# Local attention: per-head norms on four 64x64 matmul tiles, their inverses put back across partition halves, and the softmax sums ahead of the normalisation

## The chip, the core and the metric

The kernel runs on one core of a Trainium2 chip, in float32. The metric is the device time of one execution in microseconds (us); a run of the kernel is one such time, and the table below gives the median of three. One execution was also recorded by the hardware profiler, and all rows shown here come from that one. The engines are TensorE (PE; its weight loads are listed as PEld), VectorE (DVE), ScalarE (ACT), GpSimd (POOL) and SyncE (SP), which issues the DMAs.

## What is computed

The reference is a sandwich of four residual blocks on a tensor of 8 sequences x 256 tokens x 128 channels: additive attention, a six-layer local attention with a gated feed-forward layer, a state space layer, and a mixture of experts. The change lies in the local attention alone. Cut to what matters, one of its six layers is:

```python
q, k, v = split(shift_tokens(x) @ Wqkv)          # 16 heads of 64
q = l2norm(q) * q_scale                          # each head's 64 values
k = l2norm(k) * k_scale
q = q * cos * scale + rotate_half(q) * sin * scale
k = k * cos / scale + rotate_half(k) * sin / scale
sim = einsum(q, look_back(k)) * 8                # windows of 32, own and previous
out = softmax(mask(sim)) @ look_back(v)
x = out @ Wo + x
x = (a * gelu(gate)) @ W2 + b2 + x               # a, gate from layer norm, W1
```

The sum of squares of a head's 64 values, and its inverse root, are what the change is about.

## The kernel before

Everything is kept transposed: channels on the 128 partitions, tokens along the free dimension. The local attention works on chunks of 512 tokens (two batches of 256, called b = 0 and 1; four chunks per layer, 24 in all) and, within a chunk, on eight pairs of heads j = 0 to 7. A pair fills the 128 partitions: one head on partitions 0 to 63, the other on 64 to 127. Queries and keys of a pair lie side by side, 512 columns each, with q first.

Each engine has its own function `slot(i, m, j, run, more, before)`, called for every chunk i and pair j in the same order by `iterations` (a loop over layers, unrolled four chunks deep, with the first and last chunks written out). An iteration below is one chunk, eight slots. The order of the calls inside `slot` is the order of that engine's queue, written out by hand; engines meet only through semaphores. The work is staggered: in slot j the scores of pair j are made, the projection and norms of pair j + 2, the transposes of pair j - 1 and the value mix of pair j - 2. The output projection and the feed-forward layer of the chunk before are spread over the slots: Wo in slots 0 to 2 (three, three and two matmuls), the layer norm's mean in slot 3 and variance in slot 4, the gate and hidden matmuls at the end of slot 5, in slot 6 and at its end, W2 in slot 7.

The steps of one pair, with the lines of the profile:

- `project` (TensorE, L470, L471): Wq and Wk times the tokens, into PSUM banks 0 and 1, 512 columns each. It waits until the Ln of the pair before has read these banks. `values` (L459) makes part of the values on two 128x64 tiles.
- `raw_copy` (ScalarE, L646, L649): copies both banks to `raw`, then writes the squares to `sq`.
- `swap` (SyncE, L405): two DMAs copy `raw` to `shuf` with neighbouring partitions exchanged.
- `norms` (TensorE, L477, L478): two matmuls of the 128x128 matrix `same_head` (ones where two channels belong to one head) with `sq`, so that each partition holds its head's sum of squares, again in banks 0 and 1.
- `inverse_norm` (ScalarE, L655, L657): Ln of both banks into `rn`, then Exp with scale -0.5 and the bias operand `con.lift`.
- `straight` (GpSimd, L749, L753): the first step, `raw` times the cosine table, overwrites `rot`, so it waits for the normalisation of the pair before; the second step adds `shuf`, which `rotate` (VectorE, L778) has by then multiplied by the sine table.
- `normalise` (VectorE, L785): `rn` times `rot` into `qk`, which the scores read.
- `scores` (TensorE, L489 and L497): two mask matmuls, then 32 small matmuls on 64x32 tiles, into banks 4 and 5, one bank for each half of the rows.
- `soft_a` (VectorE, L793, L797): maximum and difference; the exponent (ScalarE, L699); `soft_b` (VectorE, L804, L807, L809): sums, reciprocal, product.
- `turn` (TensorE, L507): four transposes; `spread` (ScalarE, L664, L665, L667): three copies into `ptz`; `mix` (TensorE, L520): 16 matmuls on four 64x64 tiles into banks 6 and 7, one bank for each half of the rows; `out_copy` (ScalarE, L674).

In the ScalarE queue of a slot the order is exponent, raw copy, squares, output copy, value copy (L639), the layer norm's parts (L696 ahead of the exponent and L711, L713 in slot 4, L716 in slot 5), Ln, Exp, spread; the gelus and two table loads stand at the start of slot 6. In the VectorE queue it is `soft_a`, `normalise` of pair j + 1, `soft_b`, then the residual and layer norm parts, then `rotate` of pair j + 2. On TensorE, `need` attaches a wait to the next instruction; `gather` makes the wait an instruction of its own:

```python
def gather(sm_, value):
    if not isinstance(value, int) or value > 0:
        pe.wait_ge(sm_, value)
        pe.sem_inc(sem["seen"], 1)
```

An fp32 matmul appears in the profile as two records, each with its own weight load.

Of the kernel before, what the change touches and what calls it, by code (L numbers as in the profile page):

```python
# [21 lines left out]
ACT = mybir.ActivationFunctionType  # L22
AX = mybir.AxisListType

B, S, C = 8, 256, 128
T = B * S
CH = 512
# [5 lines left out]
UNIT = 512  # L33
# [11 lines left out]
def view(buf, col, *pattern, p0=0, rows=128):  # L45

    a = buf[p0:p0 + rows, 0:1]
    return bass.AP(a.tensor, a.offset + col, [[a.ap[0][0], rows]] + [list(x) for x in pattern])
# [240 lines left out]
def need(eng, sem, value):  # L289

    if not isinstance(value, int) or value > 0:
        eng.wait_ge(sem, value)


def local_attention(nc, io, x, con):
# [9 lines left out]
    with Pool(nc) as m:  # L305
# [3 lines left out]
        ps = m.mem.enter_context(nc.psum_tensor("f_ps", [128, 8 * CH], F32))  # L309
# [4 lines left out]
        fcol = m.sb("f_fcol", 9)  # L314
        base_c, base_s = m.sb("f_basec", 2 * S), m.sb("f_bases", 2 * S)
        tab_c, tab_s = m.sb("f_tabc", 2 * S), m.sb("f_tabs", 2 * S)
        same_head, ident = m.sb("f_same", C), m.sb("f_ident", C)
# [2 lines left out]
        identb = m.mem.enter_context(nc.sbuf_tensor("f_identb", [128, C], mybir.dt.bfloat16))  # L320

        v = m.sb("f_v", 8 * CH)
        raw, sq, shuf, rot, rn = (m.sb(f"f_{n}", 2 * UNIT) for n in ("raw", "sq", "shuf", "rot", "rn"))
        KOFF = UNIT + WIN
        qk = [m.sb(f"f_qk{b}", KOFF + UNIT) for b in range(2)]
        s = [m.sb(f"f_s{b}", UNIT) for b in range(2)]
# [6 lines left out]
        sem = {n: m.sem("f_" + n) for n in (  # L333
            "const wv0 wv1 wqk0 wqk1 wo w1 w2 zero flat v_mm v a_mm raw sq n_mm ln rn shuf turned straight rot qk s_mm max "
            "shift exp sum rcp p t_mm ptz pv_mm o wo_mm y1 mean cen sq2 var ln2 rs2 scaled xn g_mm gelu h_mm hid "
            "w2_mm y2 fcol tab seen").split()}
        bank = lambda k, n=1: view(ps, k * CH, *([[CH, n]] if n > 1 else []), [1, CH])


# [103 lines left out]
        def _(pe):  # L443
# [29 lines left out]

            def norms(i, j):

                need(pe, sem["sq"], i * 8 + j + 1)
                pe.matmul(bank(0), same_head[:, :], sq[:, 0:UNIT], start=True, stop=True)  # L477
                pe.matmul(bank(1), same_head[:, :], sq[:, UNIT:], start=True, stop=True).then_inc(sem["n_mm"], 1)  # L478

            def scores(i, j):  # L480

# [151 lines left out]
        def _(act):  # L633
# [17 lines left out]
            def inverse_norm(i, j):  # L651

                need(act, sem["n_mm"], i * 8 + j + 1)
                need(act, sem["qk"], i * 8 + j)
                act.activation(view(rn, 0, [UNIT, 2], [1, UNIT]), bank(0, 2), ACT.Ln, scale=float(2.0 ** 20)).then_inc(sem["ln"], 1)  # L655
                need(act, sem["ln"], i * 8 + j + 1)
                act.activation(rn[:, :], rn[:, :], ACT.Exp, scale=-0.5, bias=con.lift).then_inc(sem["rn"], 1)  # L657

            def spread(i, j):

# [102 lines left out]
        def _(dve):  # L763
# [48 lines left out]
            def hidden(i, f):  # L812

                n = FB[f][1]
                need(dve, sem["h_mm"], i * 3 + f + 1)
                need(dve, sem["gelu"], i * 3 + f + 1 + G0)
                dve.scalar_tensor_tensor(out=hid[0:n, f * UNIT:f * UNIT + UNIT], in0=view(ps, 3 * CH, [1, CH], rows=n),
                                         scalar=fcol[0:n, 2 + f:3 + f], in1=gate[0:n, f * UNIT:f * UNIT + UNIT],
                                         op0=ALU.add, op1=ALU.mult).then_inc(sem["hid"], 1)

            def slot(i, m, j, run, more, before):
# [7 lines left out]
                    hidden(k, 0)  # L829
                if before and j == 7:  # L830
                    hidden(k, 2)
                if next1:
                    normalise(u1, a1)
                if j == 6 and more and m == NU - 1:
                    tables(i + 1)
                if run:
                    soft_b(i, j)
                if before and j == 6:
                    hidden(k, 1)
                if before and j == 2:  # L840
                    need(dve, sem["wo_mm"], k + 1)
                    for g in range(2):
                        ins = dve.tensor_tensor(tokens(mk, g), tokens(mk, g), pair_of(ps, 3 * CH, 64 * g, 64), ALU.add)
# [25 lines left out]
            for t in qk:  # L869
                mm = dve.memset(t[:, UNIT:KOFF], 0.0)  # L870
# [820 lines left out]
```

## Time and profile before

| | |
|---|---|
| three runs | 2463.16, 2466.7, 2469.34 us (median 2466.7) |
| profiled execution | 2463.6 us, span 2461.8 us |
| mean granted TensorE clock | 0.971 of full speed |
| TensorE busy | 2236.4 us (91% of the span) |
| ScalarE busy | 1762.5 us (72%) |
| VectorE busy | 1596.1 us (65%) |
| GpSimd busy | 1082.4 us (44%) |
| weight loads (PEld) | 1067.3 us (43%) |

The local attention lasts from about 100 to 1925 us of the span. Its iterations take 75.6 us each with little scatter, so one iteration can stand for all. Times in a timeline are microseconds from the start of the span; busy time says that an instruction was under way, and matmul records overlap, so a busy TensorE need not be at its full rate.

### The profile page before, as it was taken

To read this page: it belongs to the slowest core of one execution; us is meant where nothing else is said; L and a number is where in the kernel's file an instruction comes from. 1 tells how busy PE (TensorE), PEld (TensorE's weight loads), DVE (VectorE), ACT (ScalarE), POOL (GpSimd) and SP (SyncE) were. 2 spreads that over 40 slices of the span, in tenths; PEclk is the share of its full clock that TensorE was granted. 3 is DMA by queue.
4 is the path that set the end of the run, shared out by engine and by line. 5 is a ranking of instruction groups with operands and counts; after the bars stand their busy time and mean duration, and the time that the engine had idled before them with its cause. 6 is when DMAs were issued, how large, how long until landed. Compare 5 with 4: busy or idle time off the path is not lost. (4 is left out here: it accounts for less than half of the span.)

```text
span 2461.8 us, 60471 instructions
## 1 busy us (share of the span) xinstructions
PE 2236.4 (91%) x24172; PEld 1067.3 (43%) x24172; DVE 1596.1 (65%) x2054; ACT 1762.5 (72%) x2574; POOL 1082.4 (44%) x461
## 2 busy tenths in 40 slices
PE   8789999999999999999999999999999687777787
PEld 3244444444444444444444444444444222222355
DVE  5556666566665666666666666766666489998442
ACT  4578877788777887777887787877787465455533
POOL 0354454444544445445454444454544015566030
PEclk8899999999999999999999999999999889999789
DMA  0211111111111112111121111211111100000001
GB/s 22 100 61 54 59 68 74 63 61 61 75 66 71 61 54 87 53 71 62 53 87 63 70 53 62 79 70 62 61 53 53 40 1 0 0 0 0 19 26 43
DMA packets 46753, 130.34 MB, mean 53 GB/s; under 512 B 9760, under 2 KB 12208, under 8 KB 46384
## 3 DMA queue, kind: packets, MB, share of 16 engines
q1 hardware_dynamic: 46480, 126.47, 13.6%
q8 instruction: 199, 3.26, 0.6%
q14 instruction: 74, 0.61, 0.1%
HBM read 24.73 MB, written 1.05 MB: 10 GB/s over the span
## 5 line engine op out<-in xcount | busy, mean ns | idle before, releaser
L749 POOL TENSOR_TENSOR f_rot<-f_raw,f_tabc 128x1024 f32<-128x1024 f32 x192 | 452.4, 2356 | 593.8 <-ACT f_raw L646 506.6
L753 POOL TENSOR_TENSOR f_rot<-f_rot,f_shuf 128x1024 f32<-128x1024 f32 x192 | 453.6, 2363 | 396.2 <-DVE f_shuf L778 396.2
L778 DVE TENSOR_TENSOR f_shuf<-f_shuf,f_tabs 128x1024 f32<-128x1024 f32 x192 | 235.4, 1226 | 306.7 <-DMA f_shuf<-f_raw 306.0
L655 ACT ACTIVATE f_rn<-f_ps 128x1024 f32<-128x1024 f32 x192 | 196.5, 1024 | 270.9 <-PE f_ps L478 270.9
L785 DVE SCALAR_TENSOR_TENSOR f_qk<-f_rn,f_rot 128x1024 f32<-128x1024 f32 x192 | 234.2, 1220 | 61.8 <-POOL f_rot L753 58.8
L477 PE MATMUL f_ps<-f_sq,f_same 128*128 128x512 f32 x384 | 205.1, 616 | 64.1 <-ACT f_sq L649 61.3
L793 DVE TENSOR_REDUCE f_max<-f_ps 128x8 f32<-128x512 f32 x192 | 132.6, 691 | 186.2 <-PE f_ps L497 185.0
L657 ACT ACTIVATE f_rn<-f_rn,k_lift 128x1024 f32<-128x1024 f32 x192 | 220.6, 1149 | 6.3
L646 ACT ACTIVATE f_raw<-f_ps 128x1024 f32<-128x1024 f32 x192 | 197.0, 1026 | 38.6 <-PE f_ps L471 37.3
L470 PE MATMUL f_ps<-y_t,f_wq 128*128 128x512 f32 x384 | 218.2, 650 | 0.6 <-ACT f_rn L655 0.4
L1172 POOL TENSOR_TENSOR s_prod<-s_state,s_cs 128x1024 f32<-128x1024 f32 x64 | 151.8, 2371 | 146.8 <-DVE s_state L1250 146.8
L459 PE MATMUL f_ps<-f_wv,y_t 128*64 128x512 f32 x768 | 208.9, 622 | 5.2 <-issue 5.2
L649 ACT ACTIVATE f_sq<-f_raw 128x1024 f32<-128x1024 f32 x192 | 203.0, 1057 | 6.1
L520 PEld LDWEIGHTS f_ps<-f_ptz,f_v 64*64 64x64 f32 x6144 | 136.2, 133 | 156.8 <-issue 156.8
L478 PE MATMUL f_ps<-f_sq,f_same 128*128 128x512 f32 x384 | 197.5, 596 | 0.0
L471 PE MATMUL f_ps<-y_t,f_wk 128*128 128x512 f32 x384 | 196.8, 594 | 0.0
L533 PE MATMUL f_ps<-f_o,f_wo 128*128 128x512 f32 x384 | 183.8, 611 | 0.0
L520 PE MATMUL f_ps<-f_ptz,f_v 64*64 64x96 f32 (+1 forms) x6144 | 162.7, 244 | 5.1 <-ACT f_ptz L667 5.1
L497 PE MATMUL f_ps<-f_qk 64*32 64x64 f32 x12288 | 165.4, 225 | 0.0
L1250 DVE TENSOR_TENSOR_SCAN s_state<-s_ps,s_state 128x1024 f32<-128x1024 f32 x64 | 146.6, 2290 | 15.0 <-ACT s_ps L1121 14.8
L1121 ACT ACTIVATE s_ps<-s_delta,s_aneg 128x1020 f32<-128x1020 f32 x64 | 71.4, 1115 | 115.5 <-DVE s_state L1250 110.1
L497 PEld LDWEIGHTS f_ps<-f_qk 64*32 64x32 f32 x12288 | 134.2, 106 | 40.8 <-issue 40.8
(264 smaller groups left out, 3684.0 us busy)
## 6 DMA issues: line engine op xcount, KB each, us to landing
f_shuf<-f_raw SPq DMA_DIRECT2D x384, 256.0 KB, 2.4
e_w<-in_e_w SPq DMA_DIRECT2D x16, 256.0 KB, 2.9
f_wq<-in_f_wq SPq DMA_DIRECT2D x12, 256.0 KB, 2.9
f_wk<-in_f_wk SPq DMA_DIRECT2D x12, 256.0 KB, 3.3
f_wv<-in_f_wv SPq DMA_DIRECT2D x12, 256.0 KB, 3.6
f_wo<-in_f_wo SPq DMA_DIRECT2D x6, 512.0 KB, 3.4
f_w<-in_f_w SPq DMA_DIRECT2D x6, 341.0 KB, 3.2
s_dx<-in_k_pick SPq DMA_DIRECT2D x1, 1536.0 KB, 9.0
```

Of the source, the lines that this page charges most:

```text
L459: mm = pe.matmul(view(ps, 2 * CH, [1, CH], p0=64 * b, rows=64), y[:, at:at + 64], wv[:, CH * (q // 4):CH * (q // 4) + CH], start=True, sto ...
L470: pe.matmul(pair_of(ps, 0), wq[:, 128 * j:128 * j + 128], shifted(m), start=True, stop=True)
L477: pe.matmul(bank(0), same_head[:, :], sq[:, 0:UNIT], start=True, stop=True)
L478: pe.matmul(bank(1), same_head[:, :], sq[:, UNIT:], start=True, stop=True).then_inc(sem["n_mm"], 1)
L497: mm = pe.matmul(view(ps, (4 + h) * CH + (2 * four + b) * 64, [1, 64], p0=WIN * (w % 4), rows=WIN), t[64 * h:64 * h + 64, WIN * w:WIN * w ...
L520: mm = pe.matmul(view(ps, (6 + b) * CH + S * b + 64 * p, [1, n], p0=64 * h, rows=64), v[64 * b:64 * b + 64, p * INNER + 128 * j + 64 * h:p ...
L649: act.activation(sq[:, :], raw[:, :], ACT.Square).then_inc(sem["sq"], 1)
L657: act.activation(rn[:, :], rn[:, :], ACT.Exp, scale=-0.5, bias=con.lift).then_inc(sem["rn"], 1)
L749: pool.tensor_tensor(view(rot, 0, [S, 4], [1, S]), view(raw, 0, [S, 4], [1, S]), view(tab_c, 0, [S, 2], [0, 2], [1, S]), ALU.mult).then_in ...
L753: pool.tensor_tensor(rot[:, :], rot[:, :], shuf[:, :], ALU.add).then_inc(sem["rot"], 1)
L778: dve.tensor_tensor(view(shuf, 0, [S, 4], [1, S]), view(shuf, 0, [S, 4], [1, S]), view(tab_s, 0, [S, 2], [0, 2], [1, S]), ALU.mult).then_i ...
L785: dve.scalar_tensor_tensor(out=view(qk[j % 2], 0, [KOFF, 2], [1, UNIT]), in0=view(rn, 0, [UNIT, 2], [1, UNIT]), scalar=1e12, in1=view(rot, ...
```

## The change

It has three parts. In `norms`, the two full matmuls become eight of 64x64: for q and k (t), for each batch (b), and for each head of the pair (h), the 64x64 block of ones times that head's 64 rows of squares, 256 columns. Batch 0's sums go to the head's own half of the partitions in bank 0; batch 1's go to the *opposite* half, in bank 1. The wait for the squares becomes a `gather`. In `inverse_norm`, `rn` is twice as wide; the Ln still covers 1024 columns; the Exp is split into one instruction for batch 0 (512 columns, 128 partitions) and two for batch 1 (512 columns, 64 partitions each), which read one half of the partitions and write the other, so that the inverse norms are back where `normalise` expects them. In the VectorE `slot`, `soft_b` of pair j comes ahead of `normalise` of pair j + 1. A semaphore named `cross` is declared and not used.

```diff
-        raw, sq, shuf, rot, rn = (m.sb(f"f_{n}", 2 * UNIT) for n in ("raw", "sq", "shuf", "rot", "rn"))
+        raw, sq, shuf, rot = (m.sb(f"f_{n}", 2 * UNIT) for n in ("raw", "sq", "shuf", "rot"))
+        rn = m.sb("f_rn", 4 * UNIT)
...
             def norms(i, j):
 
-                need(pe, sem["sq"], i * 8 + j + 1)
-                pe.matmul(bank(0), same_head[:, :], sq[:, 0:UNIT], start=True, stop=True)
-                pe.matmul(bank(1), same_head[:, :], sq[:, UNIT:], start=True, stop=True).then_inc(sem["n_mm"], 1)
+                gather(sem["sq"], i * 8 + j + 1)
+                for t in range(2):
+                    for b in range(2):
+                        for h in range(2):
+                            to = 64 * h if b == 0 else 64 - 64 * h
+                            mm = pe.matmul(view(ps, CH * b + S * t, [1, S], p0=to, rows=64),
+                                           same_head[64 * h:64 * h + 64, 64 * h:64 * h + 64],
+                                           sq[64 * h:64 * h + 64, UNIT * t + S * b:UNIT * t + S * b + S], start=True, stop=True)
+                mm.then_inc(sem["n_mm"], 1)
...
                 need(act, sem["n_mm"], i * 8 + j + 1)
                 need(act, sem["qk"], i * 8 + j)
-                act.activation(view(rn, 0, [UNIT, 2], [1, UNIT]), bank(0, 2), ACT.Ln, scale=float(2.0 ** 20)).then_inc(sem["ln"], 1)
+                act.activation(view(rn, 0, [UNIT, 4], [1, S]), view(ps, 0, [S, 4], [1, S]), ACT.Ln, scale=float(2.0 ** 20)).then_inc(sem["ln"], 1)
                 need(act, sem["ln"], i * 8 + j + 1)
-                act.activation(rn[:, :], rn[:, :], ACT.Exp, scale=-0.5, bias=con.lift).then_inc(sem["rn"], 1)
+                act.activation(view(rn, 0, [UNIT, 2], [1, S]), view(rn, 0, [UNIT, 2], [1, S]), ACT.Exp, scale=-0.5, bias=con.lift)
+                for h in range(2):
+                    of = 64 - 64 * h
+                    ins = act.activation(view(rn, S, [UNIT, 2], [1, S], p0=64 * h, rows=64),
+                                         view(rn, 2 * UNIT, [UNIT, 2], [1, S], p0=of, rows=64), ACT.Exp, scale=-0.5,
+                                         bias=con.lift_t[of:of + 64, 0:1])
+                ins.then_inc(sem["rn"], 1)
...
                 if before and j == 7:
                     hidden(k, 2)
+                if run:
+                    soft_b(i, j)
                 if next1:
                     normalise(u1, a1)
                 if j == 6 and more and m == NU - 1:
                     tables(i + 1)
-                if run:
-                    soft_b(i, j)
                 if before and j == 6:
                     hidden(k, 1)
```

## Rows read from the trace of the kernel before

**Rows 1.** Busy time by stretch: an iteration, then slots 3, 4, 5 and 6.
```profile
core 0: us, PE busy (x) PEld busy (x) DVE busy (x) ACT busy (x) POOL busy (x), PEclk, DMA share, GB/s
930.53:1006.14 75.61, 73.33 (x953) 35.70 (x950) 51.35 (x72) 60.25 (x90) 37.76 (x17) 1.00 0.21 78
1034.16:1042.07 7.91, 7.91 (x119) 3.99 (x117) 6.37 (x9) 6.61 (x11) 4.71 (x2) 1.00 0.18 69
1042.07:1050.36 8.29, 8.17 (x118) 3.91 (x116) 5.69 (x8) 8.19 (x14) 4.72 (x2) 1.00 0.28 94
1050.36:1059.89 9.53, 8.84 (x121) 4.30 (x119) 6.62 (x9) 9.04 (x13) 4.71 (x2) 1.00 0.22 87
1059.89:1072.12 12.23, 10.75 (x124) 4.86 (x122) 6.71 (x9) 10.37 (x16) 4.71 (x2) 1.00 0.11 44
```

**Rows 2.** Timeline of TensorE, slot 1: start, duration, line, operation, tiles, count.
```profile
1017.83 1.02 PE L471 MATMUL f_ps<-y_t,f_wk 128*128 128x512 f32 x2
1018.78 1.08 PE L459 MATMUL f_ps<-f_wv,y_t 128*64 128x512 f32 x4
1019.79 0.84 PE L520 MATMUL f_ps<-f_ptz,f_v 64*64 64x96 f32 x32
1020.56 2.84 PE L533 MATMUL f_ps<-f_o,f_wo 128*128 128x512 f32 x6
1023.24 1.02 PE L477 MATMUL f_ps<-f_sq,f_same 128*128 128x512 f32 x2
...
1024.95 0.60 PE L507 MATMUL f_ps<-f_ident,f_s 128*128 128x128 f32 x4
1025.39 0.38 PE L489 MATMUL f_ps<-f_maskb,f_identb 128*128 128x256 bf16 x2
```

**Rows 3.** Timeline of TensorE, slots 5 and 6: the norm matmuls, idle time before.
```profile
1055.91 1.12 PE L477 MATMUL f_ps<-f_sq,f_same 128*128 128x512 f32 x2 [0.69 <-ACT f_sq L649]
...
1069.00 1.13 PE L477 MATMUL f_ps<-f_sq,f_same 128*128 128x512 f32 x2 [1.48 <-ACT f_sq L649]
```

**Rows 4.** Timeline of ScalarE, slots 5 and 6.
```profile
1053.74 1.03 ACT L646 ACTIVATE f_raw<-f_ps 128x1024 f32<-128x1024 f32 x1
...
1056.72 0.81 ACT L716 ACTIVATE f_xn<-f_xn,f_fcol 128x512 f32<-128x512 f32 x1
1057.93 1.02 ACT L655 ACTIVATE f_rn<-f_ps 128x1024 f32<-128x1024 f32 x1 [0.40 <-PE f_ps L478]
...
1066.84 1.02 ACT L646 ACTIVATE f_raw<-f_ps 128x1024 f32<-128x1024 f32 x1 [0.15 <-PE f_ps L471]
```

**Rows 5.** Timeline of ScalarE and TensorE near the end: a late value mix.
```profile
1912.37 0.45 ACT L667 ACTIVATE f_ptz<-f_ps,f_halves 128x224 f32<-128x224 f32 x1
...
1913.12 0.62 PE L520 MATMUL f_ps<-f_ptz,f_v 64*64 64x96 f32 x10 [1.42 <-ACT f_ptz L667]
```

**Rows 6.** Timeline of ScalarE, from the end of slot 3 through slot 4.
```profile
1041.83 1.02 ACT L655 ACTIVATE f_rn<-f_ps 128x1024 f32<-128x1024 f32 x1 [1.23 <-PE f_ps L478]
1042.89 1.15 ACT L657 ACTIVATE f_rn<-f_rn,k_lift 128x1024 f32<-128x1024 f32 x1
...
1045.41 0.61 ACT L699 ACTIVATE f_ps<-f_s 128x512 f32<-128x512 f32 x1
1045.93 1.03 ACT L646 ACTIVATE f_raw<-f_ps 128x1024 f32<-128x1024 f32 x1
...
1048.91 0.69 ACT L711 ACTIVATE f_sq<-f_ps,k_eps 128x512 f32<-128x512 f32 x1
...
1050.17 1.01 ACT L655 ACTIVATE f_rn<-f_ps 128x1024 f32<-128x1024 f32 x1
```

**Rows 7.** Waits, whole span: us in total, times, longest.
```profile
POOL f_rot L753 <- DVE f_shuf L778: 396.2, 192, 3.5
```

**Rows 8.** Timeline of VectorE, slot 4: normalise and the softmax product.
```profile
1045.91 1.23 DVE L785 SCALAR_TENSOR_TENSOR f_qk<-f_rn,f_rot 128x1024 f32<-128x1024 f32 x1 [1.21 <-POOL f_rot L753]
...
1048.01 0.69 DVE L809 TENSOR_TENSOR f_s<-f_ps,f_rcp 128x512 f32<-128x512 f32 x1
```

**Rows 9.** Busy time by stretch: a loop boundary and the slot behind it.
```profile
470.95:484.29 13.34, 11.29 (x121) 5.28 (x121) 7.38 (x10) 7.92 (x12) 5.62 (x3) 0.87 0.12 44
```

More of the change, by code:

```diff
@@ L335, in local_attention @@
             "shift exp sum rcp p t_mm ptz pv_mm o wo_mm y1 mean cen sq2 var ln2 rs2 scaled xn g_mm gelu h_mm hid "
-            "w2_mm y2 fcol tab seen").split()}
+            "w2_mm y2 fcol tab seen cross").split()}
         bank = lambda k, n=1: view(ps, k * CH, *([[CH, n]] if n > 1 else []), [1, CH])
```

## The prediction, made before the change was run

> **What bounds it now.** I read the busy shares by stretch first, slot by slot through an iteration of the local attention (a slot is one head pair of one chunk, from its mask matmuls to the next slot's) [rows 1]. TensorE is busy 73.33 of an iteration's 75.61 us and ScalarE 60.25, but the slots differ. Slots 3 to 6 take 7.91, 8.29, 9.53 and 12.23 us; the other four share 75.61 - 37.96 = 37.65. The timeline of TensorE in slot 1 shows matmuls back to back up to the next slot's masks [rows 2]: in slots 0, 1, 2 and 7 TensorE is the bound. In slot 4 ScalarE's busy time is 8.19 of 8.29 us [rows 1]; in slots 5 and 6 TensorE waits 0.69 and 1.48 us for the squares that the norm matmuls sum [rows 3]. There a ring decides: Ln of one norm, Exp, spread, softmax exponent, raw copy, square, norm matmuls, next Ln. So each term is worth its full size only where its engine is the bound: TensorE in four slots, the ring in four.
>
> **Part 1, the norm matmuls (TensorE).** Two fp32 matmuls of 512 columns take 1024.95 - 1023.24 = 1.71 us [rows 2]: four records of 0.428. After, there are 16 records of 256 columns, 0.214 each, on four 64x64 tiles. The nearest row is the value mix, also four 64x64 tiles: its 32 records, 0.84 us from the first start to the last end, give the engine to Wo after 0.77 [rows 2], eight rounds of under 0.10, where 96 columns at the rate above need 0.08. So its four tiles run at once, and I take four rounds of 0.214 = 0.86 us. A change of the tile shape is not free. Wk's matmuls (128x128) to the values (128x64) take 0.95 where a pair of 0.428 is 0.86 [rows 2]: +0.09 going in. The values take 1.01, two tiles at once: +0.05 for a first weight load that nothing hides and +0.10 going out. Three Wo matmuls after the mix take 2.68, not 2.57: +0.11 for their first load. Sum 0.86 + 0.35 = 1.21 against 1.71: **-0.49 us per slot** (unrounded) where TensorE is the bound. Bounds: without those 0.35 -0.85; with them doubled -0.14. I keep them, as they were read from the same kinds of change.
> For a norm that waited, first matmul to Ln is 1057.93 - 1055.91 = 2.02 us [rows 3, 4]; four rounds shorter by 0.214 each give about 1.15. From its first matmul to the next slot it was 1072.12 - 1069.00 less the 0.86 of a hidden matmul between [rows 1, 3], 2.26; after, as in the slots that TensorE bounds (2.15 - 0.49 - 0.09 before the first matmul), 1.56.
> The wait for the squares becomes an instruction of its own ahead of the weight load. Raw copy to norm matmul is 1055.91 - 1053.74 = 2.17 with the old wait [rows 3, 4]. The mix, with two such separate waits, starts 1913.12 - 1912.82 = 0.30 after the copy that releases it [rows 5]. So one costs between 0 and 0.15; I take the middle, 0.07: raw copy to norm 2.24.
>
> **Part 2, the inverse norms (ScalarE).** Ln keeps its 1024 columns. One Exp of 1024 columns, 1.15 us, becomes three of 512, two of them on 64 partitions, which I don't expect to shorten them. The nearest row is the Ln with a bias operand on 512 columns, 0.69 us [rows 6]; the softmax exponent of 0.61 is followed after 0.52 [rows 6], so neighbours overlap by 0.09. 3 x 0.60 - (1.15 - 0.09) = **+0.74 us of ScalarE in every slot**. Bounds: as the softmax exponent, which has no bias operand, 3 x 0.52 gives +0.51; without overlap 3 x 0.69 gives +1.02. No row copies from one half of the partitions to the other; I take that as free, and the upper bound carries it.
>
> **Part 3, the softmax sums before normalise (VectorE).** The product comes earlier, normalise later. Behind normalise queues GpSimd's first step, which overwrites the rotated tensor. But GpSimd's second step waited for VectorE's rotate all 192 times, 396.2 us in total [rows 7], 2.06 each: that covers a first step up to 2 us later. Normalise, sums and product take 1048.70 - 1045.91 = 2.79 us together [rows 8]; in slot 3 the exponent will end 4.0 us after the slot's start, so normalise ends at 6.8, before the next slot's scores at 7.7. I cost the order at 0; without that cover the scores would slip by what is missing. No DMA is added or moved, and SP's queue is untouched.
>
> **The sum, slot by slot.** Ln starts 0.24 us before the next slot (1041.83 against 1042.07) [rows 1, 6]; after, 1.56 - 1.15 = 0.42 (unrounded).
> - Slots 0, 1, 2, 7: -0.49 each, -1.96. They come to 8.92 on average, slot 2 with one Wo matmul less to 8.3; the ring would allow 7.7 (next line), so TensorE still decides.
> - Slot 3: Ln to raw copy was 1053.74 - 1050.17 = 3.57 [rows 4, 6], so 4.31; raw copy to norm 2.24; norm to slot 1.56. From -0.42: 7.69, was 7.91: -0.22.
> - Slot 4 has one more square (Ln to raw copy 1045.93 - 1041.83 = 4.10 [rows 6], so 4.84): -0.42 + 4.84 + 2.24 + 1.56 = 8.22, was 8.29: -0.07. But raw copy to the next Ln is all ScalarE, 1050.17 - 1045.93 = 4.24 [rows 6], so that Ln starts at 8.66, 0.44 into slot 5 (was 0.19 before it).
> - Slot 5: raw copy at 0.44 + 4.31 = 4.75. The scaled input of the gate matmuls is finished 1057.53 - 1053.74 = 3.79 after it [rows 4]: 8.54. The norm's own matmuls end before that, so the gates wait: 8.59 + 2 x 0.86 = 10.31, was 9.53: +0.78.
> - Slot 6: its Ln starts at 8.54 - 10.31 = -1.77. Ln to raw copy was 1066.84 - 1057.93 = 8.91, 0.15 of it waiting [rows 4]; after, 8.76 + 0.74 = 9.50. Norm at -1.77 + 9.50 + 2.24 = 9.97, then 1.56 + 0.86: 12.39, was 12.23: +0.16.
> Sum -1.96 - 0.22 - 0.07 + 0.78 + 0.16 = -1.31 us an iteration. 22 full iterations give -28.8; the first, without feed-forward work, and the last, an estimate of -1.2: **-30 us**. The profiled execution took 2463.6 (its span 2461.8 and 1.8 around it): 2433.6 after. The runs' median, 2466.7, is 3.1 above it; the forecast is made against that: **2437 us**.
> With Exp at +0.51 the four ring slots gain up to 0.23 more each, 20 us: 2417. With +1.02 they lose 0.28 more each, 25 us: 2462. Half of the 0.35 going wrong moves five slots by 0.17, 19 us; the unknown of 0.07 moves two, 3 us.
>
> **Rivals.**
> *The row halves exclude each other in a bank: slower.* The four tiles write both PSUM banks from both row halves of the array. If two row halves may not write one bank together, two tiles run at once and a norm has eight rounds, +0.86. Slots 0, 1, 2, 7 lose 0.86 - 0.49 = 0.37 each; by the steps above slots 3 to 6 lose 0.66, 0.80, 0.76 and 0.55: +4.3 an iteration, +94 in 22, **2561 us**. It decides from +0.3 us per norm. For it: in the mix and the scores each row half has a bank of its own, so no row shows the new layout. Against it: two tiles that share a bank here write different partitions, and the values run two tiles into one bank at 1.01 us [rows 2], though from the same rows. The Trainium skill speaks for this rival: "TensorEngine Tiling (Array Packing)", Gotcha 1, says that different row tiles cannot access the same PSUM bank simultaneously; by it the time would be the 2561 above. Its page "PSUM — Partial Sum Buffer", on bank collisions, narrows that to the same bank and 32 partitions, which these tiles never share. Chance 0.07.
> *ScalarE's part is larger* (Exp near its upper bound, or crossing the halves has a price): no change, 2457 to 2470. Against it: the row of 0.69. Chance 0.09.
> *The clock falls.* TensorE's wait in slot 6 grows from 1.48 to about 1.9 us. In the stretch that begins with 2.03 us of idle TensorE at a loop boundary, the mean granted clock is 0.87 of full over 13.34 us [rows 9], a loss of 1.73; after waits of 1.48 the iteration's clock stays 1.00 [rows 1, 3]. If every slot 6 did it: 22 x 1.73 = +38, **2475**. In a few iterations it would cost a few us. Chance 0.07.
> *More gain than the range*, by halves that cost less: 0.05.
>
> **How the numbers follow.** The forecast has 0.72. About 0.3% (7 us) is what a measurement here can tell from no change. Faster: the forecast, the larger gain, and the milder parts of the ScalarE and clock rivals, 0.72 + 0.05 + 0.04 = 0.81. Slower: the bank rival and the clock rival's worst, 0.07 + 0.03 = 0.10. Same: 0.09. The range, 2415 to 2460, runs from the lower Exp bound to nearly the upper one; the bank rival and the clock's worst lie outside.
>
> **What would show it.** Right: 16 norm records per slot, some 1.0 us from the first to the transposes; three Exp of about 0.7 us each; slots 0, 1, 2, 7 shorter by half a microsecond, slot 3 at 7.7, slot 5 longer, at 10.3; GpSimd's second step still waiting for rotate. Wrong: norms of 1.9 us (bank), Exp on halves over 0.9 or under 0.55, a granted clock under 1.00 in slot 6, or scores that wait for normalise.

## The result and the profile after

The change made the kernel slower: 2506.3 us (median of four, 2504.2 to 2508.7) against 2464.9 in runs of the kernel before on the same chip, a ratio of 1.0171 with a 95% interval of 1.0155 to 1.0187. The forecast was 2437, its range ended at 2460, and slower had a chance of 0.10. The profiled execution took 2506.6 us, 43.0 more than that of before. These two lines are the page's first ones:

```profile
span 2504.8 us, 65656 instructions
PE 2152.6 (86%) x26476; PEld 1033.0 (41%) x26476; DVE 1776.7 (71%) x2054; ACT 1971.5 (79%) x2958; POOL 1080.8 (43%) x461
```

TensorE is busy 83.8 us less than before, as the change meant, ScalarE 209.0 more (192 norms at 1.09) and VectorE 180.6 more, for which no work was added. Line numbers have moved by up to 13: the norms are L482, Ln L662, the three Exps L664 and L667, rotate L791, GpSimd's two steps L762 and L766.

The busy times by stretch, one iteration, slots 0 to 7 in order (length, then the busy time of PE, weight loads, DVE, ACT and POOL, and the granted clock), answer to [rows 1]:

```profile
1647.99:1657.35 9.36, 9.15 (x135) 4.46 (x132) 7.38 (x10) 7.85 (x13) 4.03 (x3) 1.00 0.15 58
1657.35:1666.71 9.36, 9.16 (x135) 4.46 (x133) 6.88 (x8) 7.74 (x13) 5.00 (x3) 1.00 0.15 59
1666.71:1675.36 8.65, 8.29 (x133) 4.08 (x131) 6.86 (x10) 7.76 (x13) 4.01 (x3) 1.00 0.16 63
1675.36:1683.54 8.18, 7.50 (x131) 3.78 (x129) 7.04 (x9) 7.75 (x13) 4.25 (x3) 1.00 0.16 66
1683.54:1692.23 8.69, 7.51 (x131) 3.79 (x129) 6.60 (x7) 8.55 (x15) 4.71 (x3) 1.00 0.17 65
1692.23:1703.13 10.90, 8.40 (x133) 4.20 (x131) 8.88 (x9) 10.74 (x17) 6.36 (x3) 1.00 0.26 99
1703.13:1715.58 12.45, 10.15 (x136) 4.71 (x135) 6.88 (x10) 11.49 (x17) 4.44 (x2) 1.00 0.10 42
1715.58:1724.66 9.08, 9.08 (x134) 4.42 (x133) 6.69 (x9) 6.98 (x12) 4.98 (x3) 1.00 0.16 61
```

Only slot 7 has the gain that four slots were to have, against this stretch of the kernel before:

```profile
996.51:1006.14 9.63, 9.63 (x122) 4.75 (x120) 6.04 (x9) 5.98 (x10) 4.73 (x3) 1.00 0.14 56
```

In slots 0 to 2 TensorE, which had no gap before (slot 1 in [rows 2]), is idle 0.21, 0.20 and 0.36 us. Slots 3 to 6 are all longer than before (7.91, 8.29, 9.53, 12.23).

ScalarE's timeline in slot 0 of another iteration (start, duration, line; "x2" are two instructions) shows why; it answers to [rows 6]:

```profile
1026.54 1.02 ACT L662 ACTIVATE f_rn<-f_ps 128x1024 f32<-128x1024 f32 x1 [1.37 <-PE f_ps L482]
1027.60 0.72 ACT L664 ACTIVATE f_rn<-f_rn,k_lift 128x512 f32<-128x512 f32 x1
1028.33 1.45 ACT L667 ACTIVATE f_rn<-f_rn,k_lift 64x512 f32<-64x512 f32 x2
1029.81 0.38 ACT L677 ACTIVATE f_ptz<-f_ps 128x256 f32<-128x256 f32 x1
```

From the first Exp to the spread (L677) pass 1029.81 - 1027.60 = 2.21 us. Before, one Exp of 1.15 started at 1042.89 [rows 6], and the spread behind it stands in this row:

```profile
1043.94 0.36 ACT L664 ACTIVATE f_ptz<-f_ps 128x256 f32<-128x256 f32 x1
```

That is 1.05 later, 1.055 unrounded, so the two overlapped by 0.09. So the three Exps cost **+1.155 us a slot**: more than the forecast's +0.74 and more than its upper bound of +1.02. Each takes 0.72, and none overlaps its neighbour.

TensorE's timeline of the next slot change and of the slot behind it answers to [rows 2]; the last line is ScalarE's last spread copy of that slot:

```profile
1034.74 1.09 PE L482 MATMUL f_ps<-f_sq,f_same 64*64 64x256 f32 x16
1035.77 0.66 PE L514 MATMUL f_ps<-f_ident,f_s 128*128 128x128 f32 x4
1036.26 0.38 PE L496 MATMUL f_ps<-f_maskb,f_identb 128*128 128x256 bf16 x2
...
1039.27 1.08 PE L460 MATMUL f_ps<-f_wv,y_t 128*64 128x512 f32 x4
1040.56 0.84 PE L527 MATMUL f_ps<-f_ptz,f_v 64*64 64x96 f32 x32 [0.21 <-issue]
...
1039.81 0.45 ACT L680 ACTIVATE f_ptz<-f_ps,f_halves 128x224 f32<-128x224 f32 x1
```

The norm's 16 records give the engine on after 1.03 us and the next slot begins 1.52 after the first: the four tiles do run at once. But the mix (L527) now waits. It needs the spread copies, which stand behind the longer Exps, and it starts 1040.56 - 1040.26 = 0.30 us after the last of them ends (1.08 after it in slots 0 to 2 before). The row puts the wait down to "issue"; in the kernel with only the Exps, below, the same wait is put down to that copy.

Last, VectorE. Its rotate has become twice as long. Here is its group of the local attention before (count, busy time and mean ns, idle time before it):

```profile
L778 DVE TENSOR_TENSOR f_shuf<-f_shuf,f_tabs 128x1024 f32<-128x1024 f32 x185 | 226.8, 1226 | 289.1 <-DMA f_shuf<-f_raw 288.4
```

And the same group after:

```profile
L791 DVE TENSOR_TENSOR f_shuf<-f_shuf,f_tabs 128x1024 f32<-128x1024 f32 x186 | 425.6, 2288 | 186.0 <-DMA f_shuf<-f_raw 185.3
```

It now runs beside GpSimd's first step, which waits for the late normalise. Here are two such meetings, GpSimd's row and VectorE's row of the timeline each time:

```profile
1024.63 2.36 POOL L762 TENSOR_TENSOR f_rot<-f_raw,f_tabc 128x1024 f32<-128x1024 f32 x1 [2.45 <-DVE f_qk L798]
1026.06 2.02 DVE L791 TENSOR_TENSOR f_shuf<-f_shuf,f_tabs 128x1024 f32<-128x1024 f32 x1 [1.59 <-DMA f_shuf<-f_raw]
...
1034.67 2.36 POOL L762 TENSOR_TENSOR f_rot<-f_raw,f_tabc 128x1024 f32<-128x1024 f32 x1 [4.08 <-DVE f_qk L798]
1035.55 2.56 DVE L791 TENSOR_TENSOR f_shuf<-f_shuf,f_tabs 128x1024 f32<-128x1024 f32 x1 [1.05 <-DMA f_shuf<-f_raw]
```

GpSimd ends at 1026.99 and 1037.03, rotate at 1028.08 and 1038.11, 1.09 and 1.08 later, whenever it began; alone it takes 1.23. So rotate does nearly nothing until GpSimd's instruction is over, while GpSimd's keeps its 2.36. The Trainium skill, "SBUF — State Buffer", section "Who interferes with whom", says that a VectorE instruction with two SBUF inputs contends with a GpSimd one that reads SBUF, that the contention is an exclusive lock, and that the order of issue decides who blocks; these times agree. GpSimd's two waits in the local attention (total, times, longest) answer to [rows 7]:

```profile
POOL f_rot L762 <- DVE f_qk L798: 647.3, 180, 7.7
POOL f_rot L766 <- DVE f_shuf L791: 228.9, 186, 1.9
```

The first step now waits for normalise nearly every time, and the second still for rotate, as forecast: 1.23 each.

So the profile offers two culprits, ScalarE's Exps and the VectorE order, and a third, TensorE's clock. The runs below separate them.

### The profile page after: what moved, and what is told of

It is laid out like the page before. It is cut to its first block and busy times, and to the rows that moved or that the text cites. A ratio compares the mean times of both kernels' runs of the same rounds, so it can differ in the third digit from the quotient of the medians.

```text
span 2504.8 us, 65656 instructions
## 1 busy us (share of the span) xinstructions
PE 2152.6 (86%) x26476; PEld 1033.0 (41%) x26476; DVE 1776.7 (71%) x2054; ACT 1971.5 (79%) x2958; POOL 1080.8 (43%) x461
## 3 DMA queue, kind: packets, MB, share of 16 engines
HBM read 24.73 MB, written 1.05 MB: 10 GB/s over the span
## 5 line engine op out<-in xcount | busy, mean ns | idle before, releaser
L762 POOL TENSOR_TENSOR f_rot<-f_raw,f_tabc 128x1024 f32<-128x1024 f32 x192 | 452.4, 2356 | 794.9 <-DVE f_qk L798 658.9
L791 DVE TENSOR_TENSOR f_shuf<-f_shuf,f_tabs 128x1024 f32<-128x1024 f32 x192 | 437.1, 2276 | 202.0 <-DMA f_shuf<-f_raw 201.3
L766 POOL TENSOR_TENSOR f_rot<-f_rot,f_shuf 128x1024 f32<-128x1024 f32 x192 | 452.4, 2356 | 237.5 <-DVE f_shuf L791 237.5
L482 PE MATMUL f_ps<-f_sq,f_same 64*64 64x256 f32 x3072 | 217.9, 399 | 115.3 <-ACT f_sq L656 115.1
L662 ACT ACTIVATE f_rn<-f_ps 128x1024 f32<-128x1024 f32 x192 | 196.3, 1023 | 135.3 <-PE f_ps L482 135.1
L817 DVE TENSOR_REDUCE f_sum<-f_ps 128x8 f32<-128x512 f32 x192 | 132.8, 692 | 214.3 <-ACT f_ps L712 214.2
L667 ACT ACTIVATE f_rn<-f_rn,k_lift 64x512 f32<-64x512 f32 x384 | 276.3, 720 | 4.8
L527 PEld LDWEIGHTS f_ps<-f_ptz,f_v 64*64 64x64 f32 x6144 | 140.8, 133 | 199.7 <-issue 199.2
L482 PEld LDWEIGHTS f_ps<-f_sq,f_same 64*64 64x64 f32 x3072 | 109.7, 135 | 265.5 <-issue 246.5
L527 PE MATMUL f_ps<-f_ptz,f_v 64*64 64x96 f32 (+1 forms) x6144 | 163.4, 243 | 43.2 <-issue 25.7
```

Of the source, the lines that this page charges most:

```text
L482: mm = pe.matmul(view(ps, CH * b + S * t, [1, S], p0=to, rows=64), same_head[64 * h:64 * h + 64, 64 * h:64 * h + 64], sq[64 * h:64 * h + 6 ...
L527: mm = pe.matmul(view(ps, (6 + b) * CH + S * b + 64 * p, [1, n], p0=64 * h, rows=64), v[64 * b:64 * b + 64, p * INNER + 128 * j + 64 * h:p ...
L667: ins = act.activation(view(rn, S, [UNIT, 2], [1, S], p0=64 * h, rows=64), view(rn, 2 * UNIT, [UNIT, 2], [1, S], p0=of, rows=64), ACT.Exp, ...
L762: pool.tensor_tensor(view(rot, 0, [S, 4], [1, S]), view(raw, 0, [S, 4], [1, S]), view(tab_c, 0, [S, 2], [0, 2], [1, S]), ALU.mult).then_in ...
L766: pool.tensor_tensor(rot[:, :], rot[:, :], shuf[:, :], ALU.add).then_inc(sem["rot"], 1)
L791: dve.tensor_tensor(view(shuf, 0, [S, 4], [1, S]), view(shuf, 0, [S, 4], [1, S]), view(tab_s, 0, [S, 2], [0, 2], [1, S]), ALU.mult).then_i ...
```

## The experiments

The expectations call the theories by letters: S, ScalarE's longer inverse norms take the gain back in the ring; V, the VectorE order does, by rotate meeting GpSimd; K, TensorE loses it, by its clock after longer waits. Each kernel ran beside the kernel before on one chip, and "iteration" is the sum of the eight slots' medians over 22 iterations (before: 75.60 us; the change: 76.71), by the starts of the mask matmuls in the trace.

| kernel | us | ratio to before, 95% interval | iteration |
|---|---|---|---|
| change with the old VectorE order | 2503.3 | 1.0145 (1.0122 to 1.0167) | 76.65 |
| only the new order | 2521.7 | 1.0210 (1.0184 to 1.0236) | 78.48 |
| only the four tiles | 2383.9 | 0.9667 (0.9645 to 0.9689) | 71.86 |
| only the three Exps | 2612.3 | 1.0586 (1.0563 to 1.0608) | 81.23 |
| tiles, crossing in Ln | 2471.2 | 1.0024 (1.0010 to 1.0038) | 75.53 |
| tiles, crossing in normalise | 2431.0 | 0.9861 (0.9844 to 0.9878) | 73.61 |
| three Exps, same half | 2499.7 | 1.0145 (1.0128 to 1.0162) | 76.70 |
| tiles and new order | 2458.3 | 0.9975 (0.9966 to 0.9985) | 75.08 |
| tiles, two full Exps | 2387.9 | 0.9695 (0.9661 to 0.9729) | 72.02 |
| as normalise, pair 5 full | **2399.7** | 0.9746 (0.9716 to 0.9777) | 72.72 |
| new order but in slot 4 | 2470.2 | 1.0022 (1.0009 to 1.0036) | 75.73 |

**The change with the old VectorE order** (rotate is back at 1224 ns):

```diff
-                if run:
-                    soft_b(i, j)
                 if next1:
                     normalise(u1, a1)
...
+                if run:
+                    soft_b(i, j)
```

> The change with VectorE's old order (normalise ahead of the softmax sums). Theory S: the three Exps cost ScalarE 2.21 us a norm, not the 1.79 of the forecast, and the ring through ScalarE sets most slots; then the order matters little, 2495 to 2510 us. Theory V: the later normalise pushes GpSimd's first step onto VectorE's rotate, which is blocked (2.28 us for 1.23), and that delays the slot; then rotate falls back to 1.23 us and the time to 2480 or less.

2503.3, within the change's own time by 3 us. Beside the other two parts the order costs almost nothing; S holds.

**Only the new order**, in the kernel before (the reverse of that diff).

> The kernel before with VectorE's new order alone. Theory S: rotate slows to about 2.2 us, hidden, time unchanged (2458 to 2472 us). Theory V: slower by 25 us or more (2490 and up).

2521.7: by itself the order costs 56 us, more than the whole change. Here V's number came, and S, which had the longer rotate hidden, falls. In the iteration only slot 5 differs, and it has two lengths. Here are the slots 5 of two iterations by stretch:

```profile
931.97:944.37 12.40, 10.54 (x120) 4.87 (x118) 9.25 (x9) 9.28 (x13) 6.90 (x4) 0.86 0.11 44
1642.49:1653.20 10.71, 8.85 (x121) 4.30 (x119) 8.89 (x9) 9.13 (x13) 5.70 (x3) 1.00 0.35 120
```

VectorE's timeline at the start of the first, and TensorE's norm in the first and in the second:

```profile
931.54 2.52 DVE L778 TENSOR_TENSOR f_shuf<-f_shuf,f_tabs 128x1024 f32<-128x1024 f32 x1 [1.09 <-DMA f_shuf<-f_raw]
933.99 0.68 DVE L856 TENSOR_TENSOR f_xn<-f_cen,f_ps 128x512 f32<-128x512 f32 x1
934.58 0.68 DVE L793 TENSOR_REDUCE f_max<-f_ps 128x8 f32<-128x512 f32 x1
935.29 0.69 DVE L797 TENSOR_TENSOR f_s<-f_ps,f_max 128x512 f32<-128x512 f32 x1
...
938.70 1.82 PE L477 MATMUL f_ps<-f_sq,f_same 128*128 128x512 f32 x2 [1.86 <-ACT f_sq L649]
...
1649.21 1.12 PE L477 MATMUL f_ps<-f_sq,f_same 128*128 128x512 f32 x2 [1.86 <-ACT f_sq L649]
```

Rotate holds VectorE's queue until 934.06; the layer norm's scaled input, the maximum and the difference stand behind it, so exponent, raw copy and square are late, and TensorE waits 1.86 us for the norm instead of 0.69 [rows 3]. That lateness is 10.71 - 9.53 = 1.18 us, in every iteration. In 14 of the 22 the granted clock then falls to its lower level, 1.2 GHz, and the slot takes 12.40: 1.69 more. The same wait of 1.86 us is followed by a fall in one iteration and by none in another. 22 x 1.18 + 14 x 1.69 = 50 us, of the 55.7 by which the 22 iterations of this execution are longer than before. It was the longest of four, which took 2514 to 2533 us at mean clocks of 0.964 to 0.959.

**Only the four tiles.** The diff is that of `norms`; Ln and Exp stay, so the second batch's inverse norms stay on the wrong partitions, and q and k mix with the batches.

> The kernel before with the norm matmuls on four tiles alone; Ln and Exp as before, so the inverse norms of the second batch stay in the opposite half and q and k of the two batches are mixed up. Theory S: the ring is shorter by 0.7 us and the four slots of TensorE by 0.5: 2380 to 2405 us. Theory V says the same of this kernel. Theory K, that the four tiles save nothing: 2460 us or more.

2383.9: the tiles alone are worth 82 us. The slots (0 to 7: 9.08, 9.09, 8.22, 7.37, 7.56, 9.88, 11.58, 9.08) lose 0.54 each where TensorE is the bound. Slot 5 alone is longer, by 0.36: slot 4 now ends 0.45 us before ScalarE comes to its Ln (before, that Ln started 0.19 ahead of the end), as the forecast's steps have it with 0.44. Part 1 stands, and the bank rival and K as a cost of the tiles fall.

**Only the three Exps**, with the full norms: the diff is that of `inverse_norm`, so part of the inverse norms land on the wrong partitions and tokens.

> The kernel before with the three Exps alone, two of them across the halves; the norms stay on the full array, so the inverse norms come out in other places. Theory S: the ring grows by 1.15 us in slots 3 to 6, 60 to 105 us in all, 2525 to 2570 us. Theory V: 2465 to 2480 us.

2612.3, 147 us slower: past S's own number. Slots 3 to 6 lose 1.04, 1.17, 1.17 and 0.91, the 1.155 of the Exps or nearly; but slots 0 to 2 lose 0.40, 0.40 and 0.54 as well, and the reason is a row of TensorE's timeline in slot 0:

```profile
1580.04 0.84 PE L521 MATMUL f_ps<-f_ptz,f_v 64*64 64x96 f32 x32 [0.32 <-ACT f_ptz L674]
```

The mix waits for the spread, which S had not counted.

**Does the crossing of the halves cost?** The change with the old order, but both Exps on 64 partitions read and write the same half (the second batch's inverses stay on the wrong head):

```diff
-                    of = 64 - 64 * h
+                    of = 64 * h
```

> As no_order (three Exps, old VectorE order), but the two Exps on 64 partitions read and write the same half, so the inverse norms of the second batch of each chunk are left on the wrong head: a change of the values only. It asks whether the missing overlap of neighbouring Exps comes from crossing the halves. If crossing costs it, the starts of the three Exps fall from 0.73 to about 0.63 us apart, ScalarE gives back 0.2 to 0.3 us a slot and the time is 2465 to 2485. If it is the form of the instruction (512 columns with a bias operand, 0.72 us however many partitions), the starts stay 0.73 apart and the time stays at 2503 within 5.

2499.7, with the same ratio to before (1.0145) as the kernel that crosses. ScalarE's timeline:

```profile
1024.67 0.72 ACT L664 ACTIVATE f_rn<-f_rn,k_lift 128x512 f32<-128x512 f32 x1
1025.30 1.44 ACT L667 ACTIVATE f_rn<-f_rn,k_lift 64x512 f32<-64x512 f32 x2
1026.76 0.38 ACT L677 ACTIVATE f_ptz<-f_ps 128x256 f32<-128x256 f32 x1
```

One overlap of 0.09 is back, at the first boundary (1025.30 - 1024.67 = 0.63); the other two are still missing. Crossing is not what costs.

**Two Exps of 512 columns on all partitions**, in the kernel with the tiles alone (same values left out of place):

```diff
-                act.activation(rn[:, :], rn[:, :], ACT.Exp, scale=-0.5, bias=con.lift).then_inc(sem["rn"], 1)
+                act.activation(rn[:, 0:UNIT], rn[:, 0:UNIT], ACT.Exp, scale=-0.5, bias=con.lift)
+                act.activation(rn[:, UNIT:], rn[:, UNIT:], ACT.Exp, scale=-0.5, bias=con.lift).then_inc(sem["rn"], 1)
```

> As the kernel with the tiles alone (inverse norms of the second batch left on the wrong partitions), but its one Exp of 1024 columns is two of 512, both on all 128 partitions. Two questions. First, do neighbouring Exps of the same partitions overlap: if yes their starts are 0.63 us apart, ScalarE is longer by about 0.2 us a slot; if not 0.73 and 0.3 to 0.4. Second, is the price of ScalarE's time in the ring constant: ln_cross pays 87 us over the tiles alone for 0.78 us a slot and no_order 119 for 1.155, some 105 us per microsecond. Theory S with a constant price: 0.2 us gives 2405, 0.4 gives 2425. If the first bit is free (slack in the ring): 2380 to 2390.

ScalarE's timeline:

```profile
1028.40 0.72 ACT L663 ACTIVATE f_rn<-f_rn,k_lift 128x512 f32<-128x512 f32 x1
1029.03 0.71 ACT L664 ACTIVATE f_rn<-f_rn,k_lift 128x512 f32<-128x512 f32 x1
1029.64 0.36 ACT L671 ACTIVATE f_ptz<-f_ps 128x256 f32<-128x256 f32 x1
```

Every boundary overlaps here: 0.63 and 0.61 us from start to start, 1029.64 - 1028.40 = 1.24 for both, +0.19 against one Exp. The time is 2387.9, only 4 us above the tiles alone: a constant price per microsecond falls, the first bit is free.

**The crossing in Ln**, one Exp of 1024 columns, old order:

```diff
-                act.activation(view(rn, 0, [UNIT, 4], [1, S]), view(ps, 0, [S, 4], [1, S]), ACT.Ln, scale=float(2.0 ** 20)).then_inc(sem["ln"], 1)
+                act.activation(view(rn, 0, [UNIT, 2], [1, S]), view(ps, 0, [S, 2], [1, S]), ACT.Ln, scale=float(2.0 ** 20))
                 for h in range(2):
                     of = 64 - 64 * h
...
+                                         view(ps, CH, [S, 2], [1, S], p0=of, rows=64), ACT.Ln, scale=float(2.0 ** 20))
...
+                act.activation(rn[:, :], rn[:, :], ACT.Exp, scale=-0.5, bias=con.lift).then_inc(sem["rn"], 1)
```

> Four-tile norms as in the change, old VectorE order, one Exp of 1024 columns as before; the halves are crossed by Ln instead, which reads the sums from PSUM and has no bias operand: one Ln of 512 columns on all partitions and two of 512 columns on 64 partitions. Theory S (what costs the change its gain is ScalarE's own time in the ring of each slot): Ln of 1024 columns is about 1.06 us, three of 512 should be about 0.61 each, so +0.5 us of ScalarE a slot if they overlap like other neighbours and +0.8 if not, against +1.155 with the three Exps. Between tiles alone (2384) and no_order (2503) that gives 2420 to 2465 by share. Rival C (crossing the halves itself is dear, whichever instruction does it): each crossing Ln over 0.8 us and 2490 or more. Rival D (ScalarE's time is not the matter, any split that has the inverses late costs the same): about 2503.

ScalarE's timeline:

```profile
1023.99 0.60 ACT L661 ACTIVATE f_rn<-f_ps 128x512 f32<-128x512 f32 x1 [2.10 <-PE f_ps L481]
1024.60 1.19 ACT L664 ACTIVATE f_rn<-f_ps 64x512 f32<-64x512 f32 x2
1025.83 1.15 ACT L668 ACTIVATE f_rn<-f_rn,k_lift 128x1024 f32<-128x1024 f32 x1
```

No overlap between the Lns either: 1025.83 - 1023.99 = 1.84 for the three, +0.78 against one Ln of 1.06. Rivals C and D fall; the time, 2471.2, is 6 above S's range. In slots 3 to 6 the iteration is 2.27 us above the tiles alone. Slots 0 to 3 lose 0.46 or 0.47 each by another wait, which stands in its list of waits:

```profile
PE f_ps L470 <- ACT f_rn L664: 74.7, 134, 1.2
```

Wq writes the banks that the crossing Lns still read.

**The crossing in normalise** (VectorE), plain Ln and Exp, old order:

```diff
-                dve.scalar_tensor_tensor(out=view(qk[j % 2], 0, [KOFF, 2], [1, UNIT]), in0=view(rn, 0, [UNIT, 2], [1, UNIT]),
-                                         scalar=1e12, in1=view(rot, 0, [UNIT, 2], [1, UNIT]),
-                                         op0=ALU.min, op1=ALU.mult).then_inc(sem["qk"], 1)
+                dve.scalar_tensor_tensor(out=view(qk[j % 2], 0, [KOFF, 2], [1, S]), in0=view(rn, 0, [S, 2], [1, S]),
+                                         scalar=1e12, in1=view(rot, 0, [UNIT, 2], [1, S]), op0=ALU.min, op1=ALU.mult)
+                for h in range(2):
+                    ins = dve.scalar_tensor_tensor(out=view(qk[j % 2], S, [KOFF, 2], [1, S], p0=64 * h, rows=64),
+                                                   in0=view(rn, UNIT, [S, 2], [1, S], p0=64 - 64 * h, rows=64), scalar=1e12,
...
+                ins.then_inc(sem["qk"], 1)
```

> Four-tile norms, old VectorE order, Ln and Exp of 1024 columns each as before; the halves are crossed by VectorE: normalise becomes one instruction for batch 0 on all partitions and two for batch 1 on 64 partitions that read the inverse norms from the opposite half, 512 columns each. ScalarE's queue is that of the kernel before. Theory S: VectorE grows by some 0.2 to 0.9 us a slot, which lies beside other work, so nearly all of the gain of the tiles stays: 2384 to 2410, faster than before by 55 us or more. Rival V2 (VectorE is part of the ring: the scores wait for normalise, and softmax for the queue behind it): 2430 or more.

2431.0: 34 us faster than before and 75 faster than the change, yet past S's 2410 and just at V2's number. Its slot 4 by stretch:

```profile
1177.93:1186.83 8.90, 7.59 (x129) 3.72 (x130) 7.53 (x12) 8.02 (x14) 4.71 (x3) 1.00 0.16 62
```

VectorE's timeline in it, and TensorE's row that ends it, the masks of slot 5:

```profile
1182.90 0.69 DVE L791 SCALAR_TENSOR_TENSOR f_qk<-f_rn,f_rot 128x512 f32<-128x512 f32 x1 [1.21 <-POOL f_rot L759]
1183.61 1.39 DVE L794 SCALAR_TENSOR_TENSOR f_qk<-f_rn,f_rot 64x512 f32<-64x512 f32 x2
...
1185.03 0.69 DVE L815 TENSOR_REDUCE f_sum<-f_ps 128x8 f32<-128x512 f32 x1
...
1186.83 0.38 PE L495 MATMUL f_ps<-f_maskb,f_identb 128*128 128x256 bf16 x2 [0.64 <-DVE f_s L820]
```

The slot is 1.34 longer than with the tiles alone. Normalise takes 1185.03 - 1182.90 = 2.13 us instead of 1.2; the softmax sums and product stand behind it in VectorE's queue, and the next slot's masks wait 0.64 us for the product. That is V2's path. Most of the rest lies earlier in the slot, where the exponent waits 0.78 us for VectorE's difference.

**Pair 5 with the full norms and the single normalise**, all else as in the last:

```diff
+                if j == 5:
+                    pe.matmul(bank(0), same_head[:, :], sq[:, 0:UNIT], start=True, stop=True)
+                    pe.matmul(bank(1), same_head[:, :], sq[:, UNIT:], start=True, stop=True).then_inc(sem["n_mm"], 1)
+                    return
```

> As dve_cross, but pair 5 keeps the full norm matmuls and the single normalise of 1024 columns, because its normalise stands in slot 4, where VectorE also has the layer norm's centring and where dve_cross lost most (8.91 us against 7.56 with the tiles alone). The norm of pair 5 is in slot 3, where TensorE is not the bound. If VectorE's queue in slot 4 is what dve_cross lost by: slot 4 falls to 7.9 to 8.3 and the time to 2405 to 2422. If the loss only moves on (the later slots or the ring through GpSimd's first step, which waits for normalise): within 8 us of 2431.

Its slots 3 and 4 by stretch:

```profile
1150.17:1158.08 7.91, 7.91 (x119) 3.99 (x117) 6.63 (x10) 6.51 (x11) 4.24 (x2) 1.00 0.17 68
1158.08:1165.96 7.88, 7.44 (x131) 3.76 (x129) 6.23 (x9) 7.67 (x13) 4.56 (x3) 1.00 0.18 70
```

Slot 4 falls to 7.88, and slot 3 pays 0.22 for the full norm: 2399.7 us, 64 faster than before and 107 faster than the change, a little below the expected 2405. With it all values stand where `scores` expects them, as in the kernel before; it is the fastest such version found.

**Why did the order cost 56 us alone and 3 in the change?** First the tiles with the new order and plain Exps (out of place as above):

> Four-tile norms with plain Ln and Exp (inverse norms of the second batch left on the wrong partitions, as in the kernel with the tiles alone), plus the change's VectorE order. It asks why the new order cost 56 us alone and 3 beside the other two parts. Theory A (the order costs only where rotate runs into GpSimd's first step and the late norms then drop the clock in slot 5; the longer Exps hide it because they make everything later than rotate): here there are no longer Exps, so the order costs 30 to 60 us: 2415 to 2445, rotate over 2 us and late in slots 5 or 6. Theory B (the four-tile norms leave slack that covers the longer rotate): within 10 us of the tiles alone, 2374 to 2394.

2458.3: 74 us above the tiles alone, past A's 60, and B falls. The tiles leave no slack for the order: slot 4 is 0.76 us longer than with the tiles alone and slot 5 1.00, and in 18 of the 22 slots 5 the clock falls as well, so that they take 12.3 to 12.5 instead of 10.88. Then the order alone, but for slot 4:

```diff
-                if run:
+                if run and j != 4:
                     soft_b(i, j)
                 if next1:
                     normalise(u1, a1)
+                if run and j == 4:
+                    soft_b(i, j)
```

> The kernel before with the change's VectorE order in seven slots and the old order in slot 4. In the kernel with the new order everywhere, slot 4's normalise is late, GpSimd's first step runs beside rotate, rotate takes 2.5 us and the layer norm's scaled input, the maximum and the exponent of slot 5 stand behind it. If the whole loss of 56 us arises at this one place: within 8 us of the kernel before, 2457 to 2473, although rotate is still long in other slots. If the longer rotates cost wherever they are: 2480 or more.

2470.2, 6 us above before, though rotate still takes 1976 ns on average. Of the 56 us, some 50 arise at one place: slot 4's normalise, behind which rotate and the layer norm of slot 5 queue. The longer rotates elsewhere cost next to nothing in this kernel: slot 5 is 0.14 longer and the others keep their length. In the change slot 5 is late anyway: with the old order it takes 10.88 us, with the new one 10.89. The exponent of slot 5 shows why, with the order alone and in the change:

```profile
936.02 0.60 ACT L699 ACTIVATE f_ps<-f_s 128x512 f32<-128x512 f32 x1 [1.08 <-DVE f_s L797]
...
1696.92 0.60 ACT L712 ACTIVATE f_ps<-f_s 128x512 f32<-128x512 f32 x1
```

With the order alone ScalarE waits 1.08 us for VectorE's difference. In the change it comes to the exponent so late, behind the Exps, that it does not wait at all: what the order adds there is hidden.

## Why the prediction failed

**Part 1, right.** Norms of 1.03 us, next slot after 1.52 (forecast 1.56), Ln after 1.15 (1.15), raw copy to norm 2.23 to 2.27 (2.24), all in the profile of the change; -0.54 a slot for the tiles alone (-0.49). The rule weighed as a rival ("TensorEngine Tiling (Array Packing)", Gotcha 1, of the Trainium skill), that row tiles cannot share a bank, does not show here for tiles that write different partitions. One reading was off without harm: slot 3 was put among the ring's slots, though TensorE was busy all of its 7.91 us [rows 1], and with the tiles alone it loses 0.54 like the others.

**Part 2, the term that failed: +0.74 of ScalarE measured +1.155.** Two things were wrong. The price of one Exp was taken 0.60 net from a Ln of 0.69 that reads PSUM; the Exp, which reads SBUF, takes 0.72. The Trainium skill, "ScalarE: Activation LUTs", section "What ACT_TABLE_LOAD costs", has 0.28 us + 0.833 ns a column with a bias operand, by which an estimate for 512 columns is 0.707: the rows agree within 0.02. And the overlap of 0.09 that neighbours show was assumed at every boundary; at the three boundaries of the instructions on 64 partitions there is none. The same section of the Trainium skill gives this overlap without an exception, which these rows do not bear out. The upper bound took that away but kept the low price, so the measured value lay outside both ends.

Put 1.155 in place of 0.74 and the forecast's own steps give 8.11, 8.64, 10.73 and 12.81 for slots 3 to 6; measured are 8.18, 8.69, 10.89 and 12.45, in sum 40.21 against 40.29. The ring's arithmetic held to 0.16 in slots 3 to 5 and was 0.36 too long in slot 6; that the sums agree so closely is in part luck. The rival "ScalarE's part is larger" named the mechanism but priced it at no more than 2470, and the chance of 0.10 for slower belonged to the bank and the clock, which are not what made it slower.

**A missing step: the mix waits for the spread.** The forecast let TensorE decide in slots 0 to 2 because the ring had room up to 7.7 us; it looked at the norm alone. The spread stands behind the Exps in the same queue, and the mix needs it in mid slot. Slots 0, 1, 2 and 7 come to 36.50 instead of 37.65 - 1.96 = 35.69.

**Part 3, wrong in its argument.** That GpSimd's second step had waited for rotate covers a late first step only if rotate is not held up by it; rotate stood still until the first step was over. Its cost in the change was still near the forecast's 0: 3 us, which the runs can hardly tell from none. That was luck of this kernel, not of the argument: alone it is 56.

**The clock.** The rival put it in slot 6; the runs show it in slot 5, behind a wait of 1.5 us in the change and of 1.9 with the new order alone. In the change it falls in 5 of the 22 slots 5 (one takes 12.33 us at a mean clock of 0.86), but the slot after it is then 0.8 shorter, so that some 3 us in all remain. The wait in slot 6 of the change is longer, 1.68, and no fall followed it.

The ledger for the profiled executions: forecast for 22 iterations -28.8; Exps 4 x 0.415 x 22 = +36.5; slots 0, 1, 2, 7: 0.82 (unrounded) x 22 = +18.0; other slots -0.08 x 22 = -1.8; iterations above the median (clock, loop boundaries) +8.8. That makes +32.7 against +33.2 measured. The first iteration adds 4.7 and the last one 5.1, where the forecast had -1.2 for the two; with them the 43.0 is complete.

**What the ScalarE time costs.** Three doses on top of the tiles, old order: +0.19, +0.78 and +1.155 us a slot lengthen slots 3 to 6 by 0.14, 2.27 and 3.80 together. Four slots times (dose - 0.2) gives 0, 2.3 and 3.8: on average 0.2 us is free, and all beyond it is paid in full. By slot the free part, read from the largest dose, is 0.35, 0.03, 0.17 and 0.30 in slots 3 to 6, and with it the other two doses come out within 0.03 in every slot. Slot 3 of the crossing Lns is no test of this, since it pays by the wait of L470; and where the room comes from is seen only in slot 3, where with the tiles alone TensorE is busy all of the 7.37 us.

## What to carry to other kernels

Before an instruction is split, price each piece with its fixed part, for its own operands, and do not count on overlap between pieces on different partitions; look for every reader behind it in its queue, not only the one on the ring. Freeing time on the engine that is the bound pays only until the next engine's ring takes over, so an extra that must be paid for it belongs on an engine with slack: here VectorE's normalise, and not in the one slot where VectorE itself is late. When an order within a queue is changed, ask which two engines' instructions will meet for the first time.

## What the runs showed of the hardware that was not expected

- Neighbouring ScalarE instructions that start on the same partitions overlap by 0.09 us (0.63 between Exps of 0.72); in the trace of the change, of the crossing Lns and of the same-half Exps, none did where the first partition of input or output changed from one instruction to the next. Every boundary in these rows fits that reading, but no run varied the first partition alone.
- Instructions on 64 partitions take what those on 128 take: 0.72 (Exp) on ScalarE, 0.69 (normalise of 512 columns) on VectorE.
- A VectorE product of two SBUF tensors stands still while a GpSimd product runs: 1.23 us alone, up to 2.56 together; GpSimd loses nothing if it came first.
- After one and the same wait on TensorE of 1.86 us (1.88 at most), in the kernel with only the new order, the granted clock fell in 14 of 22 iterations and stayed in the others. A mean granted clock of 0.86 in such a slot is worth 1.7 us, and whether it falls is not to be read from the length of the wait.
